# A decoder layer with an expert stage: PSUM banks of the cross attention dealt three to the maxima and four to everything else

## What is computed

```python
x = x + self_attention_with_relative_bias(layernorm(x))     # 16 heads of 8
x = x + xattn(layernorm(x), ctx)                            # ctx: 8 x 1601 x 128
x = x + top2_of_8_experts(layernorm(x))

# inside xattn: cross attention, then self attention, then a feed-forward, each with a norm
scores = einsum('bqhd,bkhd->bhqk', q, k) / sqrt(8) + mask   # mask is 0
probs  = softmax(scores)                                    # over 1601 context rows
out    = einsum('bhqk,bkhd->bqhd', probs, v)
```

## Time and profile before

| | |
|---|---|
| median of 3 executions | 1356.24 us (1354.02 to 1360.37) |
| the profiled execution | 1356.2 us, its span 1354.4 us |
| mean granted TensorE clock over the span | 0.923 of full speed |
| busy over the span | PE 1127.9 us (83%), DVE 1018.5 (75%), ACT 883.1 (65%), POOL 358.4 (26%) |
| first and last score matmul of the cross attention's loop (line 1249) | 259.4 and 889.8 us |
| first and last grain matmul (line 1231) | 244.7 and 874.8 us |
| grain matmul, score matmul | 340 ns, 269 ns (median) |
| reduction of a grain | 565 ns (median) |
| exponential of a bank | 597 ns (median) |

### The profile page before, as it was taken

The page is one execution under the profiler, slowest core; times in us unless marked ns, Lnnn a source line. Parts: engine busy times, 40 slices in busy tenths (PEclk is TensorE's granted clock), DMA queues, the critical chain, the costliest instruction groups (busy, mean ns, idle before and its releaser), DMA issues. The chain is left out here.

```text
span 1354.4 us, 33507 instructions
## 1 busy us (share of the span) xinstructions
PE 1127.9 (83%) x12100; PEld 610.2 (45%) x12100; DVE 1018.5 (75%) x2792; ACT 883.1 (65%) x1789; POOL 358.4 (26%) x792
## 2 busy tenths in 40 slices
PE   5799976799999999999999999954788769768983
PEld 2344434244444444444444444432344346457873
DVE  7488857689888898988889899845899655555554
ACT  3488863287878878787787878833688525433443
POOL 3211115050230504114040320022122141135652
PEclk8699997699999999999999999987799869768997
DMA  6960007313231322323223031005700022101113
GB/s 164 215 138 22 2 4 179 99 40 101 76 81 48 75 68 60 96 58 76 64 67 85 17 90 40 2 1 142 132 15 2 2 94 72 53 20 38 42 39 110
DMA packets 76507, 92.34 MB, mean 68 GB/s; under 512 B 8319, under 2 KB 62567, under 8 KB 76344
## 3 DMA queue, kind: packets, MB, share of 16 engines
q1 hardware_dynamic: 72248, 83.90, 24.8%
q0 software_dynamic: 2496, 5.12, 1.4%
q10 hardware_dynamic: 1600, 1.18, 0.3%
HBM read 64.37 MB, written 27.02 MB: 67 GB/s over the span
## 5 line engine op out<-in xcount | busy, mean ns | idle before, releaser
L1447 DVE TENSOR_REDUCE MG<-bank 128x1 f32<-128x401 f32 (+1 forms) x1024 | 515.5, 567 | 73.8 <-PE bank L1231 72.0
L1367 ACT ACTIVATE PT<-bank 128x512 f32<-128x512 f32 (+1 forms) x624 | 334.8, 597 | 64.0 <-PE bank L1249 63.6
L1249 PE MATMUL bank<-QP,KP 54*128 54x256 bf16 (+1 forms) x1664 | 252.4, 273 | 16.2 <-DVE CAT L1462 4.1
L1231 PE MATMUL bank<-KP,QP 54*128 54x401 bf16 (+1 forms) x1024 | 236.7, 344 | 14.2 <-DMA KP<-ctx_k_parts 9.0
L1269 PE MATMUL bank<-PT,VP 128*9 128x256 f32 (+1 forms) x2688 | 197.1, 366 | 0.8 <-ACT XT L1367 0.8
L1249 PEld LDWEIGHTS bank<-QP,KP 54*128 54x128 bf16 (+1 forms) x1664 | 110.5, 96 | 108.1 <-ACT PT L1367 24.6
L1522 POOL TENSOR_TENSOR MP<-MN,ZERO 128x4 bf16<-128x4 f32 x128 | 26.6, 208 | 439.4 <-DVE MN L1454 434.4
L1231 PEld LDWEIGHTS bank<-KP,QP 54*128 54x128 bf16 x1024 | 75.5, 94 | 124.2 <-DVE MG L1447 95.9
L1367 ACT ACTIVATE XT<-bank 128x512 f32<-128x512 f32 (+1 forms) x208 | 116.2, 599 | 19.8 <-PE bank L1249 19.4
L900 PE MATMUL bank<-QP,KP 51*128 51x256 bf16 x512 | 94.9, 279 | 33.8 <-DVE MN L1001 9.0
L867 PE MATMUL bank<-KP,QP 51*128 51x256 bf16 x512 | 98.3, 289 | 20.9 <-PEq L113 18.8
(11 more groups left out here) (278 smaller groups left out, 2025.6 us busy)
## 6 DMA issues: line engine op xcount, KB each, us to landing
KP<-ctx_k_parts SPq DMA_DIRECT2D x128, 100.1 KB
ctx_k_parts<-KPARTS SPq DMA_DIRECT2D x16, 600.4 KB
KP<-ctx_k_parts SPq DMA_DIRECT2D x128, 59.4 KB
CN<-in_ctx SPq DMA_DIRECT2D x8, 768.0 KB
QP<-q_parts SPq DMA_DIRECT2D x22, 192.0 KB
RAW<-in_w_gate_up SPq DMA_DIRECT2D x8, 512.0 KB, 3.9
ctx_k_parts<-KPARTS SPq DMA_DIRECT2D x16, 200.1 KB
UQ<-bias_table SPq DMA_DIRECT2D x4, 768.0 KB, 8.9
```

Of the source, the lines that this page charges most:

```text
L1231: nc.tensor.matmul(GRAIN[n % NG][:, 0:w], k.QP[half, p, b * S + 128 * qt:b * S + 128 * (qt + 1)], k.KP[half, p, a:a + w], start=True, stop ...
L1249: return nc.tensor.matmul(bank[0:rows[t], S * at:S * (at + 1)], k.KP[half, p, 128 * t:128 * t + rows[t]], k.QP[half, p, b * S:(b + 1) * S] ...
L1367: nc.scalar.activation(PT[n % NP][0:rows[t], :], bank_of("s", g, t)[0:rows[t], :], ACT.Exp).then_inc(exp_done, 1)
L1447: nc.vector.tensor_reduce(MG[:, g % 4, 2 * s + qt, chunk:chunk + 1], GRAIN[n % NG][:, 0:w], AX.X, ALU.max).then_inc(m_read, 1)
```

## The change

The first ring (`GRAIN`) gets banks 0 to 2, the second (`RING`) banks 3, 4, 5 and 7. Grain n waits for the reduction of grain n - 3, and an item of the second ring for the reader of the item four turns back. The prologue, which needs four banks for its groups, takes banks 0 to 2 and bank 6 (`k.PO`), which the loop does not use before its first burst. No instruction is added or removed, and the order on every engine is as before.

```diff
-    GRAIN, RING = k.BANK[0:4], [k.BANK[4], k.BANK[5], k.PX]
-    NG = len(GRAIN)
+    GRAIN, RING = k.BANK[0:3], k.BANK[3:6] + [k.PX]
+    PRO = k.BANK[0:3] + [k.PO]
+    NG, NR = len(GRAIN), len(RING)
...
-        return RING[turn[what, unit, i] % 3]
+        return RING[turn[what, unit, i] % NR]
...
-                if n >= 3:
-                    old, a, j = TURNS[n - 3]
+                if n >= NR:
+                    old, a, j = TURNS[n - NR]
...
-                return RING[n % 3]
+                return RING[n % NR]
...
-                    last = nc.tensor.matmul(GRAIN[g][:, 128 * j:128 * (j + 1)], k.CAT[:, 128 * t:128 * (t + 1)],
+                    last = nc.tensor.matmul(PRO[g][:, 128 * j:128 * (j + 1)], k.CAT[:, 128 * t:128 * (t + 1)],
...
-                    last = nc.tensor.transpose(GRAIN[g][:, 128 * j:128 * (j + 1)], k.Y[:, 4 * g + j, :], k.ID[:, :])
+                    last = nc.tensor.transpose(PRO[g][:, 128 * j:128 * (j + 1)], k.Y[:, 4 * g + j, :], k.ID[:, :])
...
-                nc.tensor.matmul(GRAIN[g][:, :], k.WQK[:, WQ["C"], :], k.XT[:, 512 * g:512 * (g + 1)],
+                nc.tensor.matmul(PRO[g][:, :], k.WQK[:, WQ["C"], :], k.XT[:, 512 * g:512 * (g + 1)],
...
-                nc.scalar.copy(k.XT[:, 512 * g:512 * (g + 1)], GRAIN[g][:, :]).then_inc(x_taken, 1)
+                nc.scalar.copy(k.XT[:, 512 * g:512 * (g + 1)], PRO[g][:, :]).then_inc(x_taken, 1)
...
-                    last = nc.scalar.activation(out, GRAIN[g][:, :], ACT.Identity, scale=SCALE,
+                    last = nc.scalar.activation(out, PRO[g][:, :], ACT.Identity, scale=SCALE,
...
-                join_and_measure(k, v, g, k.X, GRAIN[g][:, :], k.X, (added, stats, meanvar, eps_added))
+                join_and_measure(k, v, g, k.X, PRO[g][:, :], k.X, (added, stats, meanvar, eps_added))
```

## The result

The changed kernel took 1383.37 us (median of 4, 1375.12 to 1385.62), the kernel before 1358.3 us in all its runs beside it; the ratio is 1.016, 95% interval 1.009 to 1.024. Run again beside other kernels it gave 1381.34 us against 1357.58, ratio 1.017 (1.014 to 1.020). 1376 us had been forecast, 1.5% slower.

The account below looks back on a forecast made before the run. PE's order from burst to burst was taken to bound the loop, with DVE's work beside it. Seven batches at +16 us and the last at +4 gave +20 us on 1356.24: 1376 us, range 1361 to 1394.

Parts of the forecast that it names:

- third burst, no preparation: Seven grains ahead of the third burst of values: the last waits for one reduction more, burst 0.48 us later.
- third burst, prepared: Steps preparing the next batch: fourth grain late, preparation piece loses its exponential wait, third burst 0.25 us later.
- third burst, short last piece: Third burst in prepared steps whose preparation piece has only one or two tiles: taken as 0.19 us later.
- first burst, steps 1 to 7: Four grains ahead: the fourth 0.75 us late, partly offset by a lost score bank wait, burst 0.25 us later.
- first burst, step 0 behind the batch sums: Batch sums ahead of the burst wait for the accumulator's copy, not for a ring: no change.
- second burst: T, K, V: Prepared steps: m no longer waits for K's or V's reader; 0.34, 0.34 and 0.64 us earlier, T taking K's value.
- seven batches: The seven batches that prepare another: +2.3 us each, 16 us together.
- last batch: Prepares nothing: five steps at +0.90 us, first some +0.5, last two some 0.4 gained each; +4 us.
- Rival 1: Score waits win: DVE's queue covers the new grain waits, only gains remain; about 1312 us, chance 0.05.
- Rival 2: Balance: prepared steps' third-burst losses and part of the first-burst losses are covered; 1356 to 1362 us, chance 0.10.
- Rival 3: Clock falls at all seven batch boundaries, 1385 us, chance 0.06; or swings through the whole loop, 1509 us, 0.01.
- the grains ahead of the first score cost nothing: Loop start: a bank's round of some 1.0 us fits under the 1.45 us DVE takes for three; no cost.

Follow-up runs that it names:

- e5: Kernel before the change, with DVE reducing only half of each grain's columns (0.36 us a reduction instead of 0.57): 1351.19 us, ratio 0.995.
- e2: Changed kernel with the second ring back at three banks, bank 3 unused, grains still in three: 1398.64 us, ratio 1.031 to the kernel before.
- e6: Changed kernel with DVE reducing only half of each grain's columns: 1331.14 us, ratio 0.979 to the kernel before.
- e3: Kernel before the change with only the prologue's part of it (accumulator's bank as fourth), both rings as before: 1356.55 us, ratio 0.999.
- e1: The changed kernel run again with no edit: 1381.34 us against 1357.58 for the kernel before, ratio 1.017.
- e4: Kernel before with all seven banks in one pool, dealt at build time by planned release: 1341.73 us, ratio 0.988.
- e8: The pool of seven banks with only the planner's costs of PE's items changed, nearer the profile: 1339.84 us, ratio 0.986 to the kernel before.
- e7: Kernel before with five banks for the grains and two for everything else: 1529.34 us, ratio 1.125.

## Why the prediction was right

Point by point, the burst moved by (from the rows above; for prepared steps and the batches from the starts of the bursts in both traces, the steps' the same in nearly all batches to 0.01 us):

| term | predicted | measured |
|---|---|---|
| third burst, no preparation | +0.48 | +0.48 |
| third burst, prepared | +0.25 | +0.25 |
| third burst, short last piece | +0.19 | +0.24 |
| first burst, steps 1 to 7 | +0.25 | +0.25 |
| first burst, step 0 behind the batch sums | 0 | 0.00 |
| second burst, no preparation | +0.17 | +0.16 |
| second burst: T, K, V | -0.34, -0.34, -0.64 | -0.32, -0.35, -0.64 |
| second burst, step 0 | +0.13 | +0.14 |
| one batch | +2.3 | +2.4 |
| seven batches | +16 | +17.0 |
| last batch | +4 | +4.1 |

- **The bound.** That the step is set by PE's order from burst to burst, with DVE's reductions beside it, was the step on which all of it stood. e5 confirms it: with 0.21 us less in each of 1024 reductions the whole gained 7 us.
- **Both signs in one change.** The missing bank and the added one were priced apart, and e2 measured them apart: +41 and -17.
- **Rival 1** (the score waits win) had its point of decision right: where the reductions are short enough the change does become a gain (e6), though at the fourth grain they are not short enough even at 0.36 us. At 0.57 us it was excluded by the rows. **Rival 2**, balance, would have needed the prepared steps' losses covered; they were there in full.
- **Rival 3**, the clock: in part. In the first profile the clock fell at one boundary, as before; in the second at three, 1.2 to 1.7 us each. With 184 us of waits for grain banks the clock stayed at 0.99 over the loop. What the Trainium skill tells of a kernel that cycled through PSUM banks (TensorE: Matmul & The Clock Gate, "A second HAM failure mode: psum-queue depth-cycling") did not come true here. Whether the change makes the falls at boundaries more frequent stays open: two profiles of the changed kernel and two of the old loop (its own and e3's, one fall each) are too few.
- **Where it was low.** The forecast was 20 us; the medians say 24 to 25, the profiled loop 21.1. The seven batches are 17.0 us longer and not 16. The last batch came out at 4.1 by two errors that cancel, which is luck: its first step lost 0.96 us where 0.5 stood, and its last two gained 0.70 and 0.64 where 0.4 each stood.
- **The first burst of all.** Another 0.6 us lies ahead of the loop (18.7 against 18.1 from first grain to first burst). The prediction's "the grains ahead of the first score cost nothing" held. m, behind such a grain, came 0.48 us later, but the first score matmul waits for ACT's copy of m, and that copy for the queries' parts to be stored (ACT idles 25 us ahead of it in both, released by the transfer q_parts<-PT). It starts 14.7 us behind the first grain in the kernel before and 14.8 in the changed one, as in these rows of the kernel before and of e1 (first grains at 244.66 and 247.94):

```profile
256.09 0.38 PE L1280 MATMUL bank<-IDB,MP 128*3 128x128 bf16 x4
...
259.38 0.39 PE L1249 MATMUL bank<-QP,KP 54*128 54x256 bf16 x1 [1.29 <-ACT QP L1375]
```

```profile
259.85 0.38 PE L1281 MATMUL bank<-IDB,MP 128*3 128x128 bf16 x4
...
262.74 0.39 PE L1250 MATMUL bank<-QP,KP 54*128 54x256 bf16 x1 [0.89 <-ACT QP L1376]
```

  The 0.6 comes behind it: from the first score to the first burst the kernel before took 3.4 us, both profiles of the changed one 4.0, with three waits of 0.2 to 0.4 us for grain banks. e2, with three grain banks and three score banks, took 4.0 too; with short reductions both kernels took 3.4 (e5, e6). So it is the grain bank's price ahead of a first burst once more. The term of the sum that failed is this one: the prediction set the first burst of step 0 to nothing because the batch sums stand ahead of it, but the first step of all has no sums, and there it cost 0.6.
- **What stays open.** The other 2 to 3 us between 21.7 and the medians are not in any stretch of which the profiles show that the change lengthened it. e1's profile has two more falls of the clock and a wait for keys, 4 us in its loop; how often these come in the executions without a profile is not known.

## What to carry to other kernels

Where one in-order engine feeds two consumers out of a fixed number of banks, the price of a bank is read at the last item ahead of each long block of the feeder: its start now, against the end of the read one bank nearer, plus what follows it up to the block. Waits summed over a row do not give it; here 24.6 us of score waits fell to 2.3 while every stretch of the steps without preparation got longer, since a grain beside them waited longer. Prices of both rings, stretch by stretch, also say when a bank should be lent rather than given: a pool dealt by expected release was 1.2 to 1.4% faster than the kernel before and, by the medians, 3% faster than the changed one.

## What the runs showed that I had not expected

- The pool of seven banks gains nothing before the first burst, since seven items are unread there at once; the fourth run's lower bound of 20 us was set without counting them.
- At boundaries of batches, where PE waits behind the sums, the granted clock falls to its lower level in some executions: e1 three times, e2 twice, the kernels before, after and e3 once each, e4, e5, e6 and e8 never. In e7, where PE is busy for 84% of the time and not for 94%, it was 0.93 over 300 us:

```profile
700.00:1000.00 300.00, 253.01 (x2660) 109.21 (x2652) 211.44 (x451) 203.40 (x401) 61.07 (x143) 0.93 0.18 49
```
